# Ten-step normalisation in place of the five-step one, with its own order of work, in a convolution and matching-pursuit kernel

## The chip, the cores and the metric

One core of a Trainium2 chip. The metric is the device time of one launch in microseconds. A core has TensorE (PE), VectorE (DVE), ScalarE (ACT), GpSimd (POOL) and SyncE (SP), each with an instruction list of its own; they meet only at semaphores.

## The reference, cut to what matters

```python
# x: (16, 64, 128, 128) float32
x = x + conv3x3_circular(_gn(x), weight)            # 64 -> 64 channels
x = x + sparse_code(_gn(x), dictionary)             # 4x4 patches of 64 channels: 1024 values, 1024 patches an image

def _gn(v, G=32, eps=1e-5):                         # groups of two channels
    m, s = mean(g), var(g)                          # over the group's 2 x 128 x 128 values
    return (g - m) / sqrt(s + eps)

# sparse_code: five rounds of matching pursuit for each patch
#   h = D^T x; k = 1..5: pick the atom with the largest |h|, extend the Cholesky factor by the
#   Gram entries of the atoms picked so far, h = h_bar - (coefficients @ Gram rows)
#   result = D @ coefficients
```

## The kernel before

An image is worked on in three consecutive periods. In period `i` the kernel convolves image `i` (8 blocks, `convolve(i, 0..7)`, each 18 matmul steps into `conv_ps`), correlates its patches with the 512 normalised atoms (8 tiles of 128 patches, `correlate`; tiles 0 to 3, group 0, in period `i`; tiles 4 to 7, group 1, in period `i + 1`), runs the five search rounds of each group over periods `i`, `i + 1` and `i + 2`, and reconstructs in period `i + 2` (two groups of eight blocks, `recon(i, 2, g, d)`). A period has ten **units**, entries `(periods back, group, round)` of `UNITS`: 0 (1,0,0), 1 (2,1,3), 2 (1,0,1), 3 (2,1,4), 4 (1,0,2), 5 (1,1,0), 6 (1,0,3), 7 (1,1,1), 8 (1,0,4), 9 (1,1,2). The last period, the **tail**, has twelve units and plans of its own.

A unit on each engine:

- ScalarE makes the absolute value of `h` for four tiles (line 644, "score"), the third and fourth only after VectorE has found the maximum of the first and second. The scores of unit n have the **places** 4n to 4n + 3.
- VectorE first extends the factor (`algebra`) and subtracts the projections (`project`, lines 880 and 888, two pairs of tiles), and then searches: `max` (line 771), `aim`, `max_index` (line 780), then writes which atoms, signs and Gram cells (lines 783 to 793).
- GpSimd gathers the Gram cells (line 489, four for each atom chosen before) and four Gram rows (line 501), in the order of the units, and adds a finished half of a group to the output (`add`, line 509) at the units named in `ADD_PLAN`.

Everything else is slotted in by tables written by hand. `SCALAR_PLAN[p]` lists what ScalarE does behind the score of place p; `VECTOR_PLAN[p]` what VectorE does inside unit p // 4, in steps of half a place (0 at its start, 1 and 1.5 after the first and second pair of `project`, 2 after the maxima, 2.5 after `aim`, 3 after `max_index`, 3.5 at its end). The names in them:

- `ev c`: eviction of convolution block c with its sum (line 595); the next block waits for it, since both halves of `conv_ps` are rewritten.
- `z t`, `h t`: normalised patches of tile t, into two buffers in turn (line 577); eviction of its correlation (line 588).
- `st p`: statistics (line 369): parts 0 to 8 for the next image's first norm, parts 9 to 17 for the second norm of this image.
- `oh g, t, j`: one-hot row of atom j of tile t (lines 553 and 556, four buffers, each free again when VectorE has used it); `ce g, pair`: VectorE adds them up to coefficient rows of two tiles (lines 676 and 682); `ct g, t`: eviction of their transposes (`turn` on TensorE, line 934; line 540).
- `re g, d`: eviction of a reconstruction into `rb` (line 565). For d = 0 and 4 it waits until the half that stood in `rb` has been added to the output.
- `co g`: the last row of the factor and the coefficients (VectorE, `coefficients`).
- `gn n`, `rt n`: VectorE's and ScalarE's steps of norm n, which is 0 for the image before its convolution and 1 after it.

TensorE's order is written out in `period`. Correlations and reconstructions share three PSUM banks (`gen_ps0` to `gen_ps2`); `BANKS` says which bank holds which, in order, and `room` waits for the eviction of the one before in the same bank.

Norm n before: ScalarE leaves mean, variance and three signed copies of the mean in `mv[:, n, :]`; `average` multiplies all five columns by the group matrix (line 1012); `root` on ScalarE makes variance and its root from the result in three instructions (lines 618 to 622); `gn_part` 1 on VectorE turns that into factor and offset in five (lines 696 to 705) and, for norm 0, scales the weights (lines 714 to 723); `bias` on TensorE (line 1017) makes the shift, which VectorE copies in `gn_part` 2 (line 729). `convolve(i, 0)` waits for the weights and for the shift.

## Time and profile before

| | us |
|---|---|
| median of 3 runs | 3541.99 (3540.3 to 3543.6) |
| the profiled run | 3542.37 |
| span of its profile | 3540.5 |
| TensorE busy | 3021.8 |
| VectorE busy | 2554.9 |
| ScalarE busy | 2387.1 |
| GpSimd busy | 1893.8 |

The span runs from the first to the last instruction in the trace; the run's own time is 1.9 us longer. An engine is busy while an instruction of it works; the rest is waiting. "[9.94 <-DVE ce L682]" in a row says that the engine had been idle for 9.94 us and that VectorE's instruction on `ce`, line 682, ended the wait. A wait costs time only where nothing else could have gone on.

### The profile page before, as it was taken

How to read it: one execution, taken by the hardware profiler on the slowest of the kernel's cores; microseconds unless marked ns; L12 is line 12 of the kernel's file. 1: busy time of each engine (PE TensorE's matmuls, PEld its weight loads, DVE VectorE, ACT ScalarE, POOL GpSimd, SP SyncE). 2: the span in 40 equal slices, each digit the busy share in tenths (PEclk: the TensorE clock that was granted, in tenths of full speed). 3: DMA queues.
4: the chain of work that ended last, by engine and by line, in shares of the span. 5: the costliest groups of instructions: out<-in, count | busy, mean ns of one | idle time of the engine just before them, and what ended most of it. 6: DMA issues, size and time to landing. Idle time of an engine off the chain costs nothing.

```text
span 3540.5 us, 34757 instructions
## 1 busy us (share of the span) xinstructions
PE 3021.8 (85%) x9424; PEld 1282.2 (36%) x9424; DVE 2554.9 (72%) x6469; ACT 2387.1 (67%) x3923; POOL 1893.8 (53%) x1869
## 2 busy tenths in 40 slices
PE   4995989799898989989898998989898998985547
PEld 1442334343333334333333433333343433332213
DVE  1137877878687787868778776878868687887881
ACT  3555776858677685767768676767867676755534
POOL 0016565646656564655646465555656555566661
PEclk9997999999999999999999999999999999997768
DMA  3433444435254443534444353445434443432232
GB/s 116 154 129 99 153 134 139 130 90 188 63 160 129 145 131 82 192 71 162 115 146 139 90 176 79 153 115 164 123 106 158 91 163 93 129 97 67 52 72 48
DMA packets 130515, 428.37 MB, mean 121 GB/s; under 512 B 55696, under 2 KB 55952, under 8 KB 105616
## 3 DMA queue, kind: packets, MB, share of 16 engines
q0 software_dynamic: 91776, 204.20, 23.6%
q1 hardware_dynamic: 38544, 221.96, 17.5%
q8 instruction: 76, 1.25, 0.1%
q14 instruction: 119, 0.97, 0.1%
HBM read 289.70 MB, written 136.31 MB: 120 GB/s over the span
## 4 chain that ended last, share of the span: by engine, by line
PE 46%; DVE 17%; ACT 11%; issue 10%; DMA 7%; POOL 7%; ACTq 0%; POOLq 0%; DVEq 0%
PE gen_ps L963 19%; PE gen_ps L975 16%; DVE u L880 7%; POOL v L489 6%; PE conv_ps L1031 6%; DMA y_rows<-rb 4%; ACT hot L553 4%; PE conv_ps L1038 3%; DMA v<-gram_rows,cell 3%; DVE top L771 3%; DVE h L888 2%; DVE idx L780 2%; ACT score L644 2%; ACT rb L565 1%; ACT junk_sums L369 1%
## 5 line engine op out<-in xcount | busy, mean ns | idle before, releaser
L489 POOL DMA_INDIRECT v<-gram_rows,cell x1280 | 1277.1, 998 | 882.9 <-DVE cell L789 512.9
L963 PE MATMUL gen_ps<-ct,dt 128*128 128x512 f32 x2048 | 960.2, 625 | 79.8 <-ACT rb L565 57.6
L975 PE MATMUL gen_ps<-dn,z 128*128 128x512 f32 x2048 | 915.5, 600 | 71.6 <-ACT h L588 51.3
L1031 PE MATMUL conv_ps<-xh,wc 128*128 128x512 f32 x1536 | 688.3, 596 | 46.2 <-ACT xa L595 45.2
L501 POOL DMA_INDIRECT u<-marked_rows,chosen x504 | 540.3, 1072 | 309.5 <-DVE chosen L785 160.6
L771 DVE MAX8 top<-score 128x8 f32<-128x512 f32 x640 | 420.5, 691 | 297.5 <-ACT score L644 281.7
L963 PEld LDWEIGHTS gen_ps<-ct,dt 128*128 128x128 f32 x2048 | 402.1, 200 | 603.6 <-issue 574.3
L975 PEld LDWEIGHTS gen_ps<-dn,z 128*128 128x128 f32 x2048 | 385.8, 192 | 568.6 <-issue 524.2
L644 ACT ACTIVATE score<-h 128x512 f32<-128x512 f32 x640 | 374.0, 600 | 296.2 <-DVE top L771 163.9
L880 DVE SCALAR_TENSOR_TENSOR u<-u,nl 128x512 f32<-128x512 f32 x748 | 512.1, 747 | 9.0 <-DMA u<-marked_rows,chosen 5.7
L565 ACT ACTIVATE rb<-gen_ps 128x512 f32<-128x512 f32 x256 | 274.4, 1100 | 273.3 <-PE gen_ps L963 186.3
L682 DVE SCALAR_TENSOR_TENSOR ce<-hot,xc,ce 128x512 f32<-128x512 f16 x512 | 363.9, 747 | 112.2 <-ACT hot L556 111.1
L1031 PEld LDWEIGHTS conv_ps<-xh,wc 128*128 128x128 f32 x1536 | 286.5, 189 | 407.7 <-issue 406.4
L780 DVE FIND_INDEX8 idx<-h 128x8 uint32<-128x520 f32 x640 | 432.1, 694 | 0.0
L553 ACT ACTIVATE hot<-count,which 128x512 f16<-128x512 f16 x512 | 360.7, 704 | 33.8 <-DVE ce L682 33.8
L556 ACT ACTIVATE hot<-hot,plus_minus 128x512 f16<-128x512 f16 x512 | 369.5, 722 | 16.6
L1040 PE MATMUL conv_ps<-xh,wq 64*64 64x512 f32 x1536 | 359.3, 597 | 0.0
L1038 PE MATMUL conv_ps<-xh,wq 64*64 64x512 f32 x1536 | 359.2, 597 | 0.0
L888 DVE SCALAR_TENSOR_TENSOR h<-u,na,h 128x512 f32<-128x512 f32 x504 | 352.9, 745 | 7.4 <-DMA u<-marked_rows,chosen 5.8
L577 ACT ACTIVATE z<-xa,fac 128x512 f32<-128x512 f32 x256 | 297.7, 1264 | 69.9 <-PE gen_ps L975 66.2
L934 PE MATMUL ct_ps<-ident,ce 128*128 128x128 f32 x512 | 99.1, 326 | 259.4 <-DVE ce L682 189.8
L595 ACT ACTIVATE xa<-conv_ps,shift 128x1024 f32<-128x1024 f32 x128 | 141.6, 1106 | 181.6 <-PE conv_ps L1040 181.6
(104 smaller groups left out, 1840.3 us busy)
## 6 DMA issues: line engine op xcount, KB each, us to landing
xh<-x_paired SPq DMA_DIRECT2D x128, 650.0 KB, 4.0
xa<-x_pairs SPq DMA_DIRECT2D x64, 1024.0 KB, 6.2
y_rows<-xa SPq DMA_DIRECT2D x64, 1024.0 KB, 5.1
y_rows<-rb POOLq DMA_DIRECT2D x64, 1024.0 KB, 8.5
v<-gram_rows,cell POOLq DMA_INDIRECT x1280, 2.4
u<-marked_rows,chosen POOLq DMA_INDIRECT x504, 3.9
dn<-atoms SPq DMA_DIRECT2D x1, 2048.0 KB, 11.5
gram_rows<-u POOLq DMA_DIRECT2D x4, 256.0 KB, 2.4
```

The costliest lines, as they stand in the source:

```text
L489: pool.indirect_dma_start(v[:, g, k - 1, j, t:t + 1], None, cells, bass.IndirectOffsetOnAxis(ap=cell[:, g, k // (KMAX - 1), j, t:t + 1], a ...
L501: pool.indirect_dma_start(kept(img, g, k, t), None, marked, bass.IndirectOffsetOnAxis(ap=chosen[:, g, t:t + 1], axis=0))\
L553: act.activation(place, count[:], ACT.Abs, bias=which[:, img % 2, g, j, t:t + 1], scale=-1.0)\
L644: act.activation(score[t % 2][:], h[:, g * T + t, 0:ATOMS], ACT.Abs).then_inc(score_ready[g], 1)
L771: dve.max(top8[:, t, :], score[t % 2][:]).then_inc(top_found[g], 1)
L780: dve.max_index(idx8[:, t, :], h[:, g * T + t, ATOMS:HW], h[:, g * T + t, :]).then_inc(located[g], 1)
L880: dve.scalar_tensor_tensor(kept(img, g, k, t), kept(img, g, j, t), nl[:, g, k - 1, j, t:t + 1], kept(img, g, k, t), ALU.mult, ALU.add).the ...
L888: dve.scalar_tensor_tensor(hh, kept(img, g, k, t), na[:, g, k, t:t + 1], hh, ALU.mult, ALU.add)\
L963: last = pe.matmul(to[:], dt_[:, a, d, :], ct[:, a, :], start=(a == 0), stop=(a == NA - 1))
L975: last = pe.matmul(to[:], z[:, t % 2, d // PATCH, d % PATCH, :], dn[:, d, :], start=(d == 0), stop=(d == ND - 1))
L1031: pe.matmul(conv_ps[:, a], wc[:, tap, a * CIN:a * CIN + P], rows[:, a + 1:a + 2 * CP:2, tap:tap + W], start=(tap == 0), stop=False)
L1038: pe.matmul(conv_ps[above, a], wq[second, tap, :], rows[second, a:a + 2 * CP - 1:2, tap:tap + W], start=False, stop=(tap == TAPS - 1))
```

## The change

It replaces the five-column average by three matmuls of one column, and moves nearly everything that the tables place.

- Norm n: `average` multiplies the mean alone. VectorE (part 1) copies the group mean, subtracts it and forms variance plus squared difference; `spread`, a new matmul, averages that; VectorE (part 2) adds eps; `root` is one square root on ScalarE; VectorE (part 3) makes factor, offset and, for norm 0, the weights in five instructions; part 4 is the copy of the shift. The input `avg_in` and the tiles `mv` and `gsc` shrink, `eps` goes, and the semaphore `gn_ready` is replaced by a first step of `gn_step`.
- Plans: `VECTOR_PLAN`, `SCALAR_PLAN`, `ADD_PLAN`, their tail versions and `BANKS` are other tables. For VectorE the steady order is the same but for the parts of the norms, `co 1` (23.5 for 24) and `ce 0, 1`, which stands behind `aim` instead of ahead of it.
- TensorE: convolution 7 stands between reconstructions (0,4) and (0,5), and the end of the period is in another order, with `spread` in it and `bias` last.

The core of the diff:

```diff
-GN_STEPS = 5
-GN_SUMS = (2, 1)
-GN_ROOT = 3
+GN_STEPS = 10
+GN_SUMS = (3, 2)
 VECTOR_PLAN = {
-    30: [("ce", 1, 1), ("gn", 1, 1)], 37.5: [("gn", 0, 1)], 39.5: [("gn", 0, 2)],
+    30: [("ce", 1, 1), ("gn", 1, 1)], 31: [("gn", 1, 2), ("gn", 1, 3)], 37: [("gn", 0, 1)],
+    39.5: [("gn", 0, 2), ("gn", 0, 3), ("gn", 0, 4)],
...
 SCALAR_PLAN = {
-    0: [("oh", 0, 0, 1), ("oh", 0, 1, 1)],
+    0: [("z", 4), ("oh", 0, 0, 1)],
...
-    27: [("re", 0, 4), ("st", 16), ("st", 17), ("ct", 1, 0)],
+    27: [("re", 0, 4), ("ev", 7), ("re", 0, 5), ("re", 0, 6), ("re", 0, 7), ("ct", 1, 0)],
...
 ADD_PLAN = {
-    4: [(0, 0)], 6: [(0, 1)], 7: [(1, 0)], 9: [(1, 1)],
+    4: [(0, 0)], 5: [(0, 1)], 7: [(1, 0)], 9: [(1, 1)],
 TAIL_VECTOR_PLAN = {
-    1.5: [(2, ("co", 0))], 10: [(2, ("ce", 0, 0))], 13.0: [(2, ("ce", 0, 1))], 24: [(2, ("co", 1))],
-    27: [(2, ("ce", 1, 0))], 33.0: [(2, ("ce", 1, 1))], 43.5: [(1, ("co", 0)), (1, ("ce", 0, 0))],
+    0: [(2, ("co", 0))], 10: [(2, ("ce", 0, 0))], 17.5: [(2, ("ce", 0, 1))], 21.5: [(2, ("co", 1))],
+    22.5: [(2, ("ce", 1, 0))], 27: [(2, ("ce", 1, 1))], 43.5: [(1, ("co", 0))], 44: [(1, ("ce", 0, 0))],
...
 BANKS = (
-    (("corr", 4), ("corr", 7), ("re", 0, 2), ("re", 0, 5), ("re", 1, 0), ("re", 1, 2), ("re", 1, 4), ("re", 1, 7)),
-    (("corr", 5), ("re", 0, 0), ("re", 0, 3), ("re", 0, 6), ("re", 1, 1), ("re", 1, 3), ("re", 1, 5), ("corr", 2)),
-    (("corr", 6), ("re", 0, 1), ("re", 0, 4), ("re", 0, 7), ("corr", 0), ("corr", 1), ("re", 1, 6), ("corr", 3)),
+    (("corr", 4), ("corr", 7), ("re", 0, 2), ("re", 0, 5), ("re", 1, 0), ("corr", 0), ("re", 1, 4), ("re", 1, 6)),
+    (("corr", 5), ("re", 0, 0), ("re", 0, 3), ("re", 0, 6), ("re", 1, 1), ("re", 1, 3), ("re", 1, 5), ("corr", 3)),
+    (("corr", 6), ("re", 0, 1), ("re", 0, 4), ("re", 0, 7), ("re", 1, 2), ("corr", 1), ("corr", 2), ("re", 1, 7)),
...
             def root(image, n):
-                gs = gsc[n]
-                act.wait_ge(gn_sum[n], at(image, GN_SUMS[n], 1))
-                act.activation(gs[:, 6:9], st_ps[:, 5 * n + 2:5 * n + 5], ACT.Square, accum_out=gs[:, 0:1]).then_inc(gn_root[n], 1)
...
+                act.wait_ge(gn_step[n], at(image, GN_STEPS, 5))
+                act.activation(gsc[n][:, 4:5], gsc[n][:, 3:4], ACT.Sqrt).then_inc(gn_root[n], 1)
...
                 if part == 1:
...
+                    dve.wait_ge(gn_sum[n], at(i, GN_SUMS[n], 1))
+                    dve.tensor_copy(gs[:, 0:1], st_ps[:, 3 * n:3 * n + 1]).then_inc(gn_step[n], 1)
                     after(2)
+                    dve.tensor_tensor(gs[:, 1:2], mv[:, n, 0:1], gs[:, 0:1], ALU.subtract).then_inc(gn_step[n], 1)
+                    after(3)
+                    dve.scalar_tensor_tensor(gs[:, 2:3], gs[:, 1:2], gs[:, 1:2], mv[:, n, 1:2], ALU.mult, ALU.add)\
                         .then_inc(gn_step[n], 1)
+                elif part == 2:
+                    dve.wait_ge(gn_sum[n], at(i, GN_SUMS[n], 2))
+                    dve.tensor_scalar(gs[:, 3:4], st_ps[:, 3 * n + 1:3 * n + 2], GN_EPS, None, ALU.add).then_inc(gn_step[n], 1)
+                elif part == 3:
+                    dve.wait_ge(gn_root[n], at(i, 1, 1))
+                    dve.reciprocal(gs[:, 5:6], gs[:, 4:5]).then_inc(gn_step[n], 1)
...
+            def spread(i, n):
+
+                pe.wait_ge(gn_step[n], at(i, GN_STEPS, 4))
+                pe.matmul(st_ps[:, 3 * n + 1:3 * n + 2], avg[:], gsc[n][:, 2:3], start=True, stop=True).then_inc(gn_sum[n], 1)
```

Where the tables move work, the order of instructions shows it. TensorE, end of a steady period, before: from reconstruction (1,6) to the next image's first convolution (lines 963 reconstruction, 975 correlation, 1017 bias, 1031 convolution).

```order
L963 MATMUL gen_ps2<-ct,dt 128x512 x4
L963 MATMUL gen_ps0<-ct,dt 128x512 x4
L975 MATMUL gen_ps1<-dn,z 128x512 x8
L1017 MATMUL conv_ps<-fac0,tap_sum 128x1
L975 MATMUL gen_ps2<-dn,z 128x512 x8
L1031 MATMUL conv_ps<-xh,wc 128x512 x6
```

The same place now (lines 968 reconstruction, 980 correlation, 1022 spread, 1027 bias, 1041 convolution).

```order
L980 MATMUL gen_ps2<-dn,z 128x512 x8
L968 MATMUL gen_ps0<-ct,dt 128x512 x4
L1022 MATMUL conv_ps<-gsc0,avg 128x1
L980 MATMUL gen_ps1<-dn,z 128x512 x8
L968 MATMUL gen_ps2<-ct,dt 128x512 x4
L1027 MATMUL conv_ps<-fac0,tap_sum 128x1
L1041 MATMUL conv_ps<-xh,wc 128x512 x6
```

Between bias and convolution stood a correlation; now they are neighbours. VectorE at the end of unit 9, before: the shift alone (line 729) between `hsel` and the solution of group 0.

```order
L789 SCALAR_TENSOR_TENSOR cell<-which 128x8
L793 SCALAR_TENSOR_TENSOR hsel<-pos,top 128x4
L729 COPY shift<-conv_ps 128x1
L802 TENSOR_TENSOR tmp_last<-nl,v 128x12
```

And now, in the same place:

```order
L798 SCALAR_TENSOR_TENSOR hsel<-pos,top 128x4
L698 TENSOR_SCALAR gsc<-conv_ps 128x1
L701 RECIPROCAL gsc<-gsc 128x1
L703 TENSOR_TENSOR gsc<-gsc 128x1
L705 TENSOR_SCALAR gsc<-gsc 128x1
L708 RECIPROCAL fac<-gsc 128x1
L710 TENSOR_SCALAR fac<-gsc,fac 128x1
L719 TENSOR_SCALAR wc<-taps,fac 128x3x128
L720 TENSOR_SCALAR wc<-taps,fac 128x3x64
L721 TENSOR_SCALAR wq<-taps,fac 128x192
L725 TENSOR_TENSOR wc<-wc,ident 64x2x64
L728 TENSOR_TENSOR wc<-wc,ident 64x64
L734 COPY shift<-conv_ps 128x1
L807 TENSOR_TENSOR tmp_last<-nl,v 128x12
```

Factor and weights of norm 0 have moved from unit 9's middle to its end. ScalarE behind eviction 3, before (`z 6`, a one-hot pair, `st 10`, `st 11`, `z 7`):

```order
L595 ACTIVATE xa0,sums1<-conv_ps,shift 128x2x512
L577 ACTIVATE z<-xa1,fac1 128x128x4 x2
L553 ACTIVATE hot<-count,which 128x512
L556 ACTIVATE hot<-hot,plus_minus 128x512
L369 ACTIVATE few1,minus_shift1<-sums1 128x4
L369 ACTIVATE junk_sums,sums1<-xa0,minus_shift1 128x1024 x2
L577 ACTIVATE z<-xa1,fac1 128x128x4 x2
```

And now the rows from unit 3's last score to `z 7` (line 639 score, 371 statistics):

```order
L639 ACTIVATE score1<-h 128x512
L553 ACTIVATE hot<-count,which 128x512
L556 ACTIVATE hot<-hot,plus_minus 128x512
L540 ACTIVATE ct<-ct_ps 128x4x128
L588 ACTIVATE h<-gen_ps0 128x512
L553 ACTIVATE hot<-count,which 128x512
L556 ACTIVATE hot<-hot,plus_minus 128x512
L371 ACTIVATE junk_sums,sums1<-xa0,minus_shift1 128x1024
L577 ACTIVATE z<-xa1,fac1 128x128x4 x2
```

`z 7` stood ahead of unit 3's scores and now stands behind them.

## Rows read from the trace of the kernel before

**Rows 1.** The page: busy time, share of the span, instructions of each engine.
```profile
PE 3021.8 (85%) x9424; PEld 1282.2 (36%) x9424; DVE 2554.9 (72%) x6469; ACT 2387.1 (67%) x3923; POOL 1893.8 (53%) x1869
```
**Rows 2.** By stretch: us, busy PE PEld DVE ACT POOL, clock, DMA share, GB/s.
```profile
1783.50:1988.20 204.70, 185.26 (x583) 78.49 (x582) 158.15 (x402) 148.07 (x244) 118.10 (x117) 0.96 0.44 129
...
3216.50:3540.50 324.00, 169.96 (x385) 75.70 (x384) 218.37 (x528) 165.38 (x237) 164.29 (x160) 0.75 0.28 62
```
**Rows 3.** Timeline of TensorE (start, us, line, shapes, idle before), 1900 to 1940.
```profile
1901.20 7.03 PE L963 MATMUL gen_ps<-ct,dt 128*128 128x512 f32 x16
1910.16 5.37 PE L963 MATMUL gen_ps<-ct,dt 128*128 128x512 f32 x8 [1.93 <-ACT rb L565]
...
1926.93 1.12 PE L934 MATMUL ct_ps<-ident,ce 128*128 128x128 f32 x4 [9.94 <-DVE ce L682]
...
1930.78 8.84 PE L963 MATMUL gen_ps<-ct,dt 128*128 128x512 f32 x16 [0.69 <-ACT ct L540]
```
**Rows 4.** The same timeline at the end of that period: bias, correlation 3, convolution 0.
```profile
1980.97 0.38 PE L1017 MATMUL conv_ps<-fac,tap_sum 64*128 64x1 f32 x2
1981.28 7.13 PE L975 MATMUL gen_ps<-dn,z 128*128 128x512 f32 x16
1988.25 1.03 PE L1031 MATMUL conv_ps<-xh,wc 128*128 128x512 f32 x2
```
**Rows 5.** Timeline of VectorE, 1969 to 1990: factor, shift, solution, first maximum.
```profile
1969.10 0.16 DVE L696 RECIPROCAL gsc<-gsc 128x1 f32<-128x1 f32 x1 [10.52 <-ACT gsc L622]
...
1970.00 0.22 DVE L705 TENSOR_SCALAR fac<-conv_ps,fac 128x1 f32<-128x1 f32 x1
...
1981.97 0.17 DVE L802 TENSOR_TENSOR tmp_last<-nl,v 128x12 f32<-128x12 f32 x1 [0.34 <-issue]
...
1986.08 0.16 DVE L863 TENSOR_TENSOR xc<-xc,tmp 128x4 f32<-128x4 f32 x1
1989.64 0.70 DVE L771 MAX8 top<-score 128x8 f32<-128x512 f32 x1 [3.40 <-ACT score L644]
```
**Rows 6.** Timeline of ScalarE, 1829 to 1832: a one-hot pair, eviction 3.
```profile
1829.22 0.71 ACT L553 ACTIVATE hot<-count,which 128x512 f16<-128x512 f16 x1
1829.96 0.72 ACT L556 ACTIVATE hot<-hot,plus_minus 128x512 f16<-128x512 f16 x1
...
1831.06 1.10 ACT L595 ACTIVATE xa<-conv_ps,shift 128x1024 f32<-128x1024 f32 x1
```
**Rows 7.** Timeline of ScalarE: a `z`, and the last two scores of unit 3.
```profile
1803.48 2.36 ACT L577 ACTIVATE z<-xa,fac 128x512 f32<-128x512 f32 x2
...
1853.42 1.20 ACT L644 ACTIVATE score<-h 128x512 f32<-128x512 f32 x2 [3.76 <-DVE top L771]
```
**Rows 8.** Timelines: GpSimd's last cell gather of unit 1; VectorE's first use.
```profile
1832.58 0.95 POOL L489 DMA_INDIRECT v<-gram_rows,cell  x1 [0.30 <-issue]
...
1840.00 0.17 DVE L802 TENSOR_TENSOR tmp<-nl,v 128x8 f32<-128x8 f32 x1 [5.08 <-DMA v<-gram_rows,cell]
```
**Rows 9.** Timelines: GpSimd's add of half (0,0); ScalarE's `re 0,4` behind its landing.
```profile
1899.43 0.98 POOL L509 DMA_DIRECT2D y_rows<-rb  x1 [4.66 <-ACT rb L565]
...
1908.93 1.08 ACT L565 ACTIVATE rb<-gen_ps 128x512 f32<-128x512 f32 x1 [3.16 <-DMA y_rows<-rb]
```
**Rows 10.** Busy time by stretch: behind the 2 us wait; around the 2.4 us one.
```profile
1910.30:1913.70 3.40, 3.40 (x5) 1.34 (x6) 2.73 (x4) 2.18 (x10) 2.77 (x3) 0.51 0.15 55
...
1855.60:1862.40 6.80, 4.41 (x29) 1.89 (x22) 6.58 (x21) 6.55 (x13) 2.72 (x3) 1.00 0.57 205
```
**Rows 11.** Timeline of TensorE in the period of image 1: correlations 1 and 2.
```profile
325.87 16.01 PE L975 MATMUL gen_ps<-dn,z 128*128 128x512 f32 x32 [15.26 <-ACT h L588]
```
**Rows 12.** Timelines in the tail: GpSimd's first gather of unit 9; VectorE's wait for them.
```profile
3385.53 0.95 POOL L489 DMA_INDIRECT v<-gram_rows,cell  x1 [1.18 <-DVE cell L789]
...
3407.40 0.17 DVE L802 TENSOR_TENSOR tmp_last<-nl,v 128x12 f32<-128x12 f32 x1 [6.23 <-DMA v<-gram_rows,cell]
```

More of the change, by code:

```diff
@@ L441, in first_statistics @@
                 statistics(act, 0, 0, part)
[L443 removed]
+        setup(nc, ctx, sem, w_taps, atoms, ident_in, avg_in, dn, taps, tap_sum, ones, count, ident, avg, plus_minus, rd,
               atoms_in, first_image, first_rows, first_statistics)
@@ L912, in period @@
                     search(i - back, g, k, between)
-            for part in (1, 2):
+            for part in (1, 2, 3, 4):
                 gn_part(0, 0, 0, part)
@@ L1093, in period @@
                     recon(i, 2, 0, 4)
-                    turn(i - 2, 1, 0)
+                if own:
+                    convolve(i, 7)
+                if p:
                     recon(i, 2, 0, 5)
@@ L1097, in period @@
                     recon(i, 2, 0, 7)
+                    turn(i - 2, 1, 0)
+                    turn(i - 2, 1, 1)
                 if own:
@@ L1100, in period @@
                 if p:
-                    turn(i - 2, 1, 1)
                     turn(i - 2, 1, 2)
                     turn(i - 2, 1, 3)
+                if own:
+                    spread(i, 1)
+                if p:
                     recon(i, 2, 1, 0)
                     recon(i, 2, 1, 1)
+                    recon(i, 2, 1, 2)
                 if own:
@@ L1117, in period @@
                     recon(i, 2, 1, 5)
-                    recon(i, 2, 1, 6)
-                    recon(i, 2, 1, 7)
                 if own:
                     correlate(i, 0, 2)
+                if p:
+                    recon(i, 2, 1, 6)
+                if here[-1]:
+                    spread(i + 1, 0)
+                if own:
+                    correlate(i, 0, 3)
+                if p:
+                    recon(i, 2, 1, 7)
                 if here[-1]:
                     bias(i + 1, 1 - par)
-                if own:
-                    correlate(i, 0, 3)
             def tail(i):
                 correlate(i, 1, 4)
+                turn(i - 2, 0, 0)
                 correlate(i, 1, 5)
-                turn(i - 2, 0, 0)
                 turn(i - 2, 0, 1)
-                turn(i - 2, 0, 2)
                 correlate(i, 1, 6)
                 correlate(i, 1, 7)
+                turn(i - 2, 0, 2)
                 turn(i - 2, 0, 3)
@@ L1181, in _ @@
             average(0, 0)
+            spread(0, 0)
             bias(0, 0)
@@ L1185, in _, with setup @@
             tail(images)
-def setup(nc, ctx, sem, w_taps, atoms, ident_in, avg_in, dn, taps, tap_sum, ones, count, ident, avg, eps, plus_minus, rd,
+def setup(nc, ctx, sem, w_taps, atoms, ident_in, avg_in, dn, taps, tap_sum, ones, count, ident, avg, plus_minus, rd,
           atoms_in, first_image, first_rows, first_statistics):
```

63 lines of the change are left out of this document (23 added, 40 removed), and 98 rows, old and new, of tables (SCALAR_PLAN, TAIL_SCALAR_PLAN, VECTOR_PLAN).

## The prediction

> **What bounds the kernel now.** I read the busy shares first, then one image in the steady state, then TensorE's idle stretches in it, and last who fed them. TensorE is busy 85% of the span, VectorE 72%, ScalarE 67% [rows 1]. One steady period (from the first convolution of an image to that of the next) takes 204.7 us, and TensorE works 185.3 us of it [rows 2]; there are 14 of them. Before them stand the periods of images 0 and 1, behind them the tail of 324.0 us, in which TensorE works 170.0 us [rows 2]. So TensorE sets the steady pace, less its waits. Below, +n is n us after the start of the period that begins at 1783.45.
>
> The waits stand close together. After the reconstructions of group 0 TensorE waits 1.93 us for a bank (`re 0,4` not yet evicted); the block behind it takes 5.37 us where others take 3.5, since the clock has fallen. Then the turns wait 9.94 us for the coefficients of the second pair, and the next two reconstructions take 8.84 us where two take 7.0 [rows 3]. From the end of reconstruction (0,7) to the start of (1,0) pass 15.4 us (1915.4 to 1930.8). Everywhere else in the period TensorE idles under 1 us at a time, but for one wait of 2.4 us.
>
> **The normalisation itself.** Per image and norm the change takes three small ScalarE instructions and the 128x3 one away, and adds five small VectorE ones of 0.16 to 0.22 us [rows 5], a matmul of the size of the average (0.3 us on TensorE) and two more crossings between engines. Bare arithmetic is about 1 us for VectorE and 0.3 us for TensorE per norm, and ScalarE gains about 0.8 us. What counts is where the steps stand.
>
> Norm 1 (of the image after its convolution) runs inside the 15.4 us hole, so I walk the hole again. Reconstruction (0,7) ends at T. Its eviction now stands ahead of `ct 1,0`: the scores of unit 7 start at T+1.4 instead of T+0.7. Statistics 16 and 17, which ran ahead of the hole, now cost ScalarE 2.6 us in it; the one-hot pair `oh 1,3,2` (1.4 us) and `re 0,5` have left it. The last two one-hot tiles are ready at T+10.8 and T+12.6, the coefficients at T+13.4, the last turn and copy end at T+15.3, `spread` passes at T+14.7, and (1,0) starts at T+15.35. So the hole stays 15.4 us; VectorE comes out about 3 us later, but what follows waits for tile 0's correlation in both orders, so I cost that at nothing (cover: `z 2` cannot start before that correlation ends, at T+34.5).
>
> Norm 0 (of the next image) now: VectorE waits 10.52 us for ScalarE's root at 1969.10 [rows 5]. In the new order its first part only needs the average, long since there; the wait goes. What is late next is the second half: scores 38 and 39 stand behind `h 2` and `re 1,6`, the search ends some 6.4 us after reconstruction (1,6), then root, factor and weights end after 9.6 us; TensorE meanwhile has correlation 3 (7.0 us) and reconstruction (1,7) (3.5 us) = 10.5 us. It fits with 0.9 us for the weights and 2.4 us for `bias`. But bias is now the last thing ahead of the convolution, and the shift is copied behind it: 0.15 + 0.15 for the extra matmuls and 0.35 for the copy. Before, bias had a correlation of 7 us as cover [rows 4]. From T to the next convolution: 72.9 us become 73.4.
>
> **The start of the period.** VectorE stands at the shift until +0 and only then solves group 0's coefficients (4.3 us; from 1981.97 to 1986.2 before, ahead of the period) [rows 5]. It used to idle 3.40 us there [rows 5], so of 4 us lag 0.5 us are left after the first search. One-hot tiles: one is made ahead of eviction 0 where three were, at 1.38 us each; the coefficients of the first pair end at +19.8 instead of +18.2. VectorE is then 1.6 us late through units 1 to 3. The wait for gathered cells (5.08 us) [rows 8] does not absorb it, since the cells are asked for 1.6 us later too.
>
> On ScalarE seven one-hot pairs instead of five (one of them held 1.0 us before) stand between unit 2's last score and eviction 3: scores end 1.8 us later, and 2 x 1.38 - 1.0 us are added. Eviction 3 started at +47.6 [rows 6] and now starts at +51.2. Convolution 4 needs it and started at +49.3 without a wait; now it waits 3.5 us, to +52.5. `z 7` was ready at +57.3 in the old list; now it stands behind unit 3's scores, `oh 1,0,2`, `ct 0,2`, `h 4`, `oh 1,1,2` and statistics 13 (together 5.0 us). Those scores started at +70.0 [rows 7], now +71.6 to +72.8; `z 7` (2.3 us [rows 7]) is ready at +80.1. Correlation 7 started at +77.0; now it waits 3.5 us and starts at +80.2.
>
> **What is given back.** From there the old order had 43.8 us of work plus a turn 0.5, the wait 1.93 and the slow block 1.9. The new one puts convolution 7 between reconstructions 4 and 5. Then `re 0,4` is the only tight eviction: `re 0,3` at +116.7, its add lands 9.5 us later (that is what `re 0,4` waited for before, 3.16 us at 1908.93) [rows 9], so `re 0,4` ends at +127.4, and (0,7) may start at +127.5, just when TensorE gets there. So T = +80.2 + 7.0 + 43.8 = +131.0, against +131.9 before.
>
> The period without clock effects: 131.0 + 73.4 = 204.4, against 204.8.
>
> **The clock.** At the 2 us wait the granted clock read 0.51 in the next 3.4 us (the 1.2 GHz level), and such a fall follows that wait in 10 of the 14 periods; around the 2.4 us wait at 1858 it stayed 1.00, in all of them [rows 10]. One fall costs 1.9 us (5.37 against 3.5) [rows 3]. The old fall goes with its wait; that is in the sum. Two new waits of 3.5 us arise. A fall behind the first is absorbed by the second; one behind the second moves T. I take half a fall, +0.9. The Trainium skill ("TensorE: Matmul & The Clock Gate", section "HAM oscillation — how this bites in real kernels") says of a kernel whose engine waits for data in each step that the clock drops each time and the return is paid again each time; the trace bears that out at the long wait of each period and not at the 2.4 us one. By the page each new wait would bring a fall: that is rival A.
>
> **Start and tail.** Image 0: `spread` and the eps step lengthen the chains, about +2 us. Image 1: TensorE waits 15.26 us for `h 0` ahead of the second correlation [rows 11], because tiles 0 and 1 share a bank. In the new bank table tile 1 takes bank 2 and tile 0 bank 0, so one correlation (7.0 us) moves into that wait: -7.0, less 0.4 for the shift. Start together -4.6. Tail: the second half of image 14's coefficients moves from units 6 and 8 to units 5 and 6. GpSimd's gathers of unit 5 are asked for behind 12.4 us of VectorE work that stood behind them, and units 7 and 9 wait for cells: the search of unit 9, which ended at 3384.9 and releases 16 gathers and then everything to the end [rows 12], comes 5 us later. Bounds: -4.5 (a wait for `h` in unit 4 that goes) and +12. I take +5.
>
> **Sum.** 14 x (204.4 + 0.9 - 204.8 = +0.5) = +7.0; start -4.6; tail +5: +7.4. The span 3540.5 becomes 3547.9; its run took 3542.4, 1.9 more, and the median of three is 3542.0, so 3550 us.
>
> **Rivals.**
> A, both clocks fall. Each period 1.9 instead of 0.9 behind the second wait and no relief: +1.4 per period, +20 in all, 3562. For it: a 2 us wait already did it in 10 of 14. Against: the first fall shortens the second wait to 1.7 us.
> B, ScalarE has no slack. From reconstruction (0,2) to `re 0,4` it has 19.6 us of work in 20.7, and the add of (0,1), one unit earlier in GpSimd's list, now holds unit 6's twelve gathers until `re 0,7` is out: they start at +133.4 instead of +126.9. The last cell took up to 6.5 us to be used [rows 8], so unit 8's algebra comes at +155.4, 5 us behind VectorE. I found it covered by `z 2` and by the 5 us after which `h 0` is first needed; a second such delay is not. If one of the two costs 3 us a period: +42, 3584.
> C, faster. The lag of 1.6 us does not arise (VectorE idles 2 to 5 us in units 0 to 3, which my walk fills too strictly), both waits shrink to under 2 us, no clock falls, and the old fall and bank wait are gone all the same: 202.8 a period, 28 us less, 3514.
> D, nothing moves: every loss is covered by the 15.4 us hole; 3542.
>
> **Chances.** Forecast 0.40, A 0.15, B 0.12, C 0.25, D 0.08. The forecast's own spread is about 12 us either way. A measurement can tell about 0.2% (7 us): below 3535 is faster, above 3549 slower. Of the forecast 0.22 lies within, 0.16 above, 0.02 below; of A 0.13 above; D within. Faster 0.27, same 0.32, slower 0.41. Range: C at the low end, B at the high one, 3512 to 3590.
>
> **What would show it.** The wait of 10.5 us before the factor of norm 0 gone, and a short wait of VectorE at the shift in its place; TensorE idle 3 to 4 us ahead of convolution 4 (for eviction 3) and ahead of correlation 7 (for `z 7`), and none ahead of reconstruction (0,7); the hole still 15 to 16 us; in image 1 the second correlation ahead of the long wait. I am wrong if the steady period differs from 205.3 by over 1.5 us, or if TensorE waits over 1 us at `bias` or the first convolution, which would mean that the search of unit 9 ends later than I walked it.

## The result, and the profile after

| | before | after |
|---|---|---|
| median of 5 runs, us | 3542.79 (3540.3 to 3543.6) | 3558.77 (3555.2 to 3562.0) |
| ratio | | 1.0046, 95% interval 1.0034 to 1.0057 |
| the profiled run, us | 3542.37 | 3555.88 |
| its span, us | 3540.5 | 3553.6 |

The changed kernel is slower by 0.46%, 16 us in the medians and 13.1 us in the two profiled spans (the run that was profiled is 2.9 us below the median of its five). By period (from the first convolution of one image to that of the next), in us:

| | before | after | difference | forecast |
|---|---|---|---|---|
| up to image 0's first convolution | 41.4 | 40.9 | -0.5 | |
| image 0 | 138.0 | 142.9 | +4.9 | +2 |
| image 1 | 169.7 | 162.0 | -7.7 | -6.6 |
| images 2 to 14, 13 periods | 2663.2 | 2675.8 | +12.6 | +6.5 |
| image 15 and the tail | 528.2 | 532.0 | +3.8 | +5.5 |

The first of the 13 went from 205.7 to 208.0. The others lay between 204.0 and 205.7; now nine take 204.8 to 205.1 and three 207.5 to 207.8.

The page's line of busy times, after, answers to [rows 1]; each engine does nearly what it did:

```profile
PE 3062.6 (86%) x9488; PEld 1307.6 (37%) x9488; DVE 2581.6 (73%) x6596; ACT 2368.8 (67%) x3795; POOL 1860.6 (52%) x1869
```

Busy time by stretch (columns as in [rows 2]): the first 6.8 us of a convolution 4 with a fallen clock, of a correlation 7 with one, of a convolution 4 without, and a whole steady period.

```profile
1633.80:1640.60 6.80, 6.79 (x9) 2.89 (x10) 2.63 (x16) 6.40 (x13) 5.20 (x6) 0.56 0.93 316
1250.00:1256.80 6.80, 6.80 (x11) 2.96 (x12) 5.89 (x11) 6.74 (x14) 5.28 (x6) 0.70 0.48 156
1221.20:1228.00 6.80, 6.80 (x28) 2.78 (x32) 2.54 (x16) 6.40 (x13) 5.25 (x6) 1.00 0.92 315
1581.40:1786.30 204.90, 187.55 (x587) 80.19 (x587) 159.97 (x411) 147.11 (x237) 115.80 (x117) 0.95 0.43 129
```

**The two kinds of period.** Timeline of TensorE in a period of 205.0 us, which begins at 1581.4 (lines 1041 convolution, 980 correlation):

```profile
1633.81 8.37 PE L1041 MATMUL conv_ps<-xh,wc 128*128 128x512 f32 x12 [3.09 <-ACT xa L595]
1644.86 7.13 PE L980 MATMUL gen_ps<-dn,z 128*128 128x512 f32 x16
...
1661.89 2.41 PE L980 MATMUL gen_ps<-dn,z 128*128 128x512 f32 x5 [0.97 <-ACT z L577]
```

and in one of 207.8 us, which begins at 1168.8:

```profile
1221.16 5.40 PE L1041 MATMUL conv_ps<-xh,wc 128*128 128x512 f32 x12 [3.09 <-ACT xa L595]
1229.23 7.13 PE L980 MATMUL gen_ps<-dn,z 128*128 128x512 f32 x16
...
1249.98 9.16 PE L980 MATMUL gen_ps<-dn,z 128*128 128x512 f32 x16 [4.58 <-ACT z L577]
```

Both wait 3.09 us ahead of convolution 4, at +52.4. In the first the clock falls: the whole convolution takes 11.1 us (1633.81 to 1644.86) where the second needs 8.1, and TensorE comes 3 us later to correlation 7, for which it would have had to wait anyway. In the second the clock stays at 1.00, the wait for `z 7` is 4.58 us, and the clock falls there, where nothing absorbs it: 9.16 us for a correlation of 7.1. With the 0.7 us by which `z 7` itself is later there (+81.2 for +80.5), that is the 2.8 us between the kinds.

**The hole.** TensorE's timeline around the end of reconstruction (0,7), at 1712.7 (+131.3), answers to [rows 3]:

```profile
1704.82 7.89 PE L968 MATMUL gen_ps<-ct,dt 128*128 128x512 f32 x18
1712.54 0.60 PE L939 MATMUL ct_ps<-ident,ce 128*128 128x128 f32 x4
1714.41 0.63 PE L939 MATMUL ct_ps<-ident,ce 128*128 128x128 f32 x4 [1.26 <-ACT ct L540]
1719.47 0.59 PE L1017 MATMUL conv_ps<-mv,avg 128*128 128x1 f32 x2 [4.44 <-ACT mv L416]
1724.36 1.12 PE L939 MATMUL ct_ps<-ident,ce 128*128 128x128 f32 x4 [4.30 <-DVE ce L677]
1726.25 1.09 PE L939 MATMUL ct_ps<-ident,ce 128*128 128x128 f32 x4 [0.78 <-DVE ce L677]
1727.13 0.43 PE L1022 MATMUL conv_ps<-gsc,avg 128*128 128x1 f32 x2
1728.03 8.21 PE L968 MATMUL gen_ps<-ct,dt 128*128 128x512 f32 x14 [0.47 <-ACT ct L540]
```

From the end of (0,7) to the start of (1,0) pass 15.3 us, as in the rows of before (1915.53 to 1930.78 in [rows 3]; the prediction's 15.4 is 0.1 high). The single wait of 9.94 us is cut in two by the average, 4.44 and 4.30 us; `spread` stands at the hole's end.

**Image 1.** TensorE's timeline there (answers to [rows 11]): the second correlation now follows the first at once, at 316.37, and only the third waits for an `h`.

```profile
306.58 9.82 PE L980 MATMUL gen_ps<-dn,z 128*128 128x512 f32 x16 [6.02 <-ACT z L577]
316.37 7.11 PE L980 MATMUL gen_ps<-dn,z 128*128 128x512 f32 x16
326.67 9.99 PE L980 MATMUL gen_ps<-dn,z 128*128 128x512 f32 x16 [3.19 <-ACT h L588]
```

**What I had not foreseen** stands in the page's group for the projection. Idle time ahead of line 885 (880 before) over the whole run, and what ended most of it, before and then after:

```profile
L880 DVE SCALAR_TENSOR_TENSOR u<-u,nl 128x512 f32<-128x512 f32 x748 | 512.1, 747 | 9.0 <-DMA u<-marked_rows,chosen 5.7
```

```profile
L885 DVE SCALAR_TENSOR_TENSOR u<-u,nl 128x512 f32<-128x512 f32 x748 | 513.9, 747 | 95.0 <-DMA u<-marked_rows,chosen 92.4
```

One period of it, after. VectorE in unit 3 (the algebra of line 807 is the first use of the gathered cells, line 885 the first of the Gram rows):

```profile
1635.11 0.21 DVE L807 TENSOR_TENSOR tmp<-nl,v 128x8 f32<-128x8 f32 x1 [0.37 <-DMA v<-gram_rows,cell]
...
1642.04 4.07 DVE L885 SCALAR_TENSOR_TENSOR u<-u,nl 128x512 f32<-128x512 f32 x6 [4.90 <-DMA u<-marked_rows,chosen]
```

GpSimd's last cell gather of unit 1 and the first and last of its row gathers:

```profile
1632.63 0.94 POOL L489 DMA_INDIRECT v<-gram_rows,cell  x1 [0.30 <-issue]
1633.88 0.94 POOL L501 DMA_INDIRECT u<-marked_rows,chosen  x1 [0.30 <-issue]
...
1637.62 0.94 POOL L501 DMA_INDIRECT u<-marked_rows,chosen  x1 [0.30 <-issue]
```

SyncE's queue: the store of group 0 of the convolved image to the output, two transfers of 1 MB.

```profile
1633.69 0.82 SPq L472 DMA_DIRECT2D y_rows<-xa  x2
```

Before, VectorE waited 5.08 us for the cells and not for the rows [rows 8], and the same store, SyncE's timeline of before, came at

```profile
1832.28 0.82 SPq L472 DMA_DIRECT2D y_rows<-xa  x2
```

which is beside the last cell gather (1832.58). The store waits for eviction 3. Whatever gathers lie behind that eviction land late: the cells before, the rows after. In the changed kernel the second half of the store lands at +60.1 to +60.2 in nine of the periods of images 3 to 14, and the first projection starts at +60.5 to +60.6; in the other three it lands at +61.1 to +61.3 and the projection starts at +61.2 to +61.4. So the row that is used first lands with the end of the store, not in the middle of it.

**Rival B** can be read here too. GpSimd's last cell gather of unit 6, and VectorE's first use in unit 8:

```profile
1730.42 0.94 POOL L489 DMA_INDIRECT v<-gram_rows,cell  x1 [0.31 <-issue]
...
1732.81 0.17 DVE L807 TENSOR_TENSOR tmp<-nl,v 128x8 f32<-128x8 f32 x1 [1.43 <-DMA v<-gram_rows,cell]
```

The add does hold unit 6's gathers, until +134.0 (forecast +133.4), but their last cell is used at +151.4 and not at +155.4; VectorE waits 1.43 us for it, and from (0,7) to the next convolution pass 73.3 to 73.9 us in all the periods of images 3 to 14, near the 73.4 that was forecast without B. The 3 us a period of rival B are not there.

### The profile page after: what moved, and what is told of

It is laid out like the page before. It is cut to its first block, busy times and chain, and to the rows that moved or that the text cites. A ratio compares the mean times of both kernels' runs of the same rounds, so it can differ in the third digit from the quotient of the medians.

```text
span 3553.6 us, 34884 instructions
## 1 busy us (share of the span) xinstructions
PE 3062.6 (86%) x9488; PEld 1307.6 (37%) x9488; DVE 2581.6 (73%) x6596; ACT 2368.8 (67%) x3795; POOL 1860.6 (52%) x1869
## 4 chain that ended last, share of the span: by engine, by line
PE 51%; DVE 14%; issue 11%; ACT 9%; POOL 9%; DMA 4%; ACTq 0%; POOLq 0%; DVEq 0%; SPq 0%
PE gen_ps L968 22%; PE gen_ps L980 15%; POOL v L489 9%; PE conv_ps L1041 8%; DVE u L885 6%; PE conv_ps L1048 4%; ACT hot L553 4%; DMA u<-marked_rows,chosen 3%; DVE h L893 2%; DVE idx L785 2%; DVE top L776 2%; ACT score L639 1%; ACT z L577 1%; ACT junk_sums L371 1%; ACT ct L540 1%
## 5 line engine op out<-in xcount | busy, mean ns | idle before, releaser
L968 PE MATMUL gen_ps<-ct,dt 128*128 128x512 f32 x2048 | 945.0, 616 | 65.5 <-ACT rb L565 56.2
L980 PE MATMUL gen_ps<-dn,z 128*128 128x512 f32 x2048 | 926.7, 606 | 50.4 <-ACT z L577 39.9
L1041 PE MATMUL conv_ps<-xh,wc 128*128 128x512 f32 x1536 | 722.2, 621 | 84.3 <-ACT xa L595 76.9
L501 POOL DMA_INDIRECT u<-marked_rows,chosen x504 | 507.6, 1007 | 305.8 <-DVE chosen L790 156.9
L1041 PEld LDWEIGHTS conv_ps<-xh,wc 128*128 128x128 f32 x1536 | 296.4, 197 | 461.5 <-issue 459.1
L509 POOL DMA_DIRECT2D y_rows<-rb x64 | 63.1, 987 | 366.4 <-ACT rb L565 366.3
```

Of the source, the lines that this page charges most:

```text
L501: pool.indirect_dma_start(kept(img, g, k, t), None, marked, bass.IndirectOffsetOnAxis(ap=chosen[:, g, t:t + 1], axis=0))\
L968: last = pe.matmul(to[:], dt_[:, a, d, :], ct[:, a, :], start=(a == 0), stop=(a == NA - 1))
L980: last = pe.matmul(to[:], z[:, t % 2, d // PATCH, d % PATCH, :], dn[:, d, :], start=(d == 0), stop=(d == ND - 1))
L1041: pe.matmul(conv_ps[:, a], wc[:, tap, a * CIN:a * CIN + P], rows[:, a + 1:a + 2 * CP:2, tap:tap + W], start=(tap == 0), stop=False)
```

## Theories

*Theory.* The order of work costs the time, through the two waits that it makes, ahead of convolution 4 (eviction 3 is late) and of correlation 7 (`z 7` stands behind unit 3's scores), and unit 3's scores are late because the store lies on its Gram rows. *Rivals.* The ten steps cost it; a late eviction 3 alone is what matters; the rows are late for a reason of their own; GpSimd's earlier add holds gathers up (B of the prediction).

## The experiments

**Order or steps.** The kernel before with the tables and TensorE's order of the changed one, and the five-step norms kept.

```diff
 VECTOR_PLAN, SCALAR_PLAN, ADD_PLAN, their tail versions, BANKS, period(): those of the changed kernel, but
-    31: [("gn", 1, 2), ("gn", 1, 3)], 37: [("gn", 0, 1)], 39.5: [("gn", 0, 2), ("gn", 0, 3), ("gn", 0, 4)],
+    31: [("gn", 1, 1)], 39.5: [("gn", 0, 1), ("gn", 0, 2)],
```

> The new tables and TensorE order with the old five-step normalisation (no spread; factor of norm 1 at place 31, factor, weights and shift of norm 0 at 39.5). If the order of work makes the difference, as I hold, this stays within 0.15% of the changed kernel: 3552 to 3560 us, steady periods of 205.0 and 207.7 us, and only image 0's period is shorter, by some 3 us (183.8 - 40.9 = 142.9 in the changed kernel). If the ten steps themselves cost the time, it falls to 3540 to 3546.

Measured: 3550.79 us, ratio to before 1.0025 (1.0015 to 1.0035). That is 1.2 us below the range of the first case and far from that of the second. The 13 steady periods read as in the changed kernel, nine at 204.7 to 205.2, three at 207.7 to 207.9, and the first at 210.7 (208.0). Image 0 takes 137.7 us instead of 142.9, image 1 160.1 instead of 162.0. So of 16 us the order costs 10 (3550.8 against 3540.8 for the kernel before on that chip) and the steps some 4 to 6, 4.3 in the profiled spans: 5.2 us in image 0. The 1.9 us of image 1 come back in image 2 (210.7 for 208.0). In the other steady periods the steps cost nothing. On this chip the kernel before took 2.0 us less than on that of the result, and 1.4 us less on the chip of the store by itself and of the version from the parts; differences to the changed kernel below are uncertain by that much.

**`z 7` earlier**, by one place of unit 3:

```diff
-    13: [("oh", 1, 1, 1)],
-    15: [("oh", 1, 0, 2), ("ct", 0, 2), ("h", 4), ("oh", 1, 1, 2), ("st", 13), ("z", 7), ("h", 5), ("h", 6),
+    13: [("oh", 1, 1, 1), ("z", 7)],
+    15: [("oh", 1, 0, 2), ("ct", 0, 2), ("h", 4), ("oh", 1, 1, 2), ("st", 13), ("h", 5), ("h", 6),
```

> The changed kernel with z 7 moved from place 15 to place 13, where ScalarE idles 4.0 us. Theory (TensorE waits for z 7 ahead of correlation 7): that wait (1.0 us where the clock fell before, 4.6 where it did not) and the fall behind it vanish, steady periods 203 to 204.2 us, total 3533 to 3545. Rival (the reconstructions are held by ScalarE and the add, so it is given back before reconstruction 0,7): 3552 to 3560, with a wait of 1 us or more ahead of (0,7).

Measured: 3532.53 us, 0.9976 (0.9967 to 0.9985). The wait ahead of correlation 7 is gone in all periods, the one of 3.1 us ahead of convolution 4 is left, and periods take 202.4 to 204.8 us (image 2's aside, 208.9). The time is half a microsecond below what was expected, and the periods spread wider on both sides. The wait of 1 us or more ahead of (0,7), the rival's sign, is there in seven of the 12 periods of images 3 to 14 (1.1 to 1.7 us), with no fall behind it.

**Eviction 3 earlier**, behind the one-hot pair `oh 0,3,3`:

```diff
-    11: [("oh", 0, 2, 2), ("oh", 0, 3, 2), ("oh", 0, 2, 3), ("oh", 0, 3, 3), ("oh", 0, 2, 4), ("oh", 0, 3, 4),
-        ("oh", 1, 0, 1), ("ct", 0, 1), ("ev", 3), ("st", 10), ("st", 11), ("st", 12), ("st", 0), ("ev", 4)],
+    11: [("oh", 0, 2, 2), ("oh", 0, 3, 2), ("oh", 0, 2, 3), ("oh", 0, 3, 3), ("ev", 3), ("oh", 0, 2, 4), ("oh", 0, 3, 4),
+        ("oh", 1, 0, 1), ("ct", 0, 1), ("st", 10), ("st", 11), ("st", 12), ("st", 0), ("ev", 4)],
```

> The changed kernel with eviction 3 three one-hot pairs and a copy earlier on ScalarE (4.6 us). The wait of 3.1 us ahead of convolution 4 goes, and the clock fall behind it. Theory (z 7 is the later bound, and the fall ahead of it only fills its wait): correlation 7 starts no earlier, waits 4.6 us in every period, the clock falls behind it in most, all steady periods 207 to 208 us, total 3570 to 3590, so slower than the changed kernel. Rival (the wait before convolution 4 is what costs): 3 us a period less, 3510 to 3520.

Measured: 3545.12 us, 1.0012 (1.0003 to 1.0021): neither of the two. The wait ahead of convolution 4 went, and TensorE waited longer for `z 7` instead, 3.7 to 4.6 us, with a fall of the clock behind it in each of the 12 periods of images 3 to 14:

```profile
1655.58 4.63 PE L980 MATMUL gen_ps<-dn,z 128*128 128x512 f32 x5 [3.78 <-ACT z L577]
```

That much was expected. But this correlation 7 starts at +76.9 to +78.5, not at +80.5, though I had taken the move for one that leaves `z 7` where it was. With eviction 3 the store is issued at +47.7 instead of +52.3, the first of the rows lands at +55.8 in the period of this row, and the projection starts at +57.2 without a wait, instead of at +60.6 after 4.9 us. This is what led to the store.

**Both** edits together, nothing else.

> Both moves. Theory: neither wait nor fall is left up to the reconstructions; steady periods 200.5 to 203 us, total 3495 to 3530, faster than the kernel before. If ScalarE's work from reconstruction (0,2) to re 0,4 and the landing of the add take it back, a wait of 2 to 4 us appears ahead of reconstruction (0,7) with a fall behind it and the total is 3535 to 3550.

Measured: 3493.73 us, 0.9871 (0.9856 to 0.9886), 1.3% faster than before, 1.3 us below the range of the theory. Apart the two edits give 26.2 and 13.7 us against the changed kernel, together 65.0: each alone leaves the other wait, and the clock falls behind that one. With both, none of TensorE's waits between +40 and the hole is over 2.1 us, no clock falls behind them, and correlation 7 starts at +73.0 to +73.9 (image 2 aside). Ahead of reconstruction (0,7) this is left:

```profile
1676.53 3.67 PE L968 MATMUL gen_ps<-ct,dt 128*128 128x512 f32 x8 [1.37 <-ACT rb L565]
```

The block takes 3.67 us, so the clock did not fall; in [rows 3] it did behind 1.93 us. In the kernel before the same wait has both outcomes: with 1.87 to 2.55 us over 14 periods the clock fell behind it in 10, and the four others (1.87, 2.02, 2.08 and 2.28 us) are not the shortest ones.

**The store by itself.** The changed kernel with one thing different: SyncE issues the store of group 0 behind convolution 4. No list of a computing engine is touched.

```diff
-                    if here[0] and (r + 1) % (ROUNDS // GROUPS) == 0:
-                        g = r // (ROUNDS // GROUPS)
-                        sp.wait_ge(x1_ready, at(i, ROUNDS, r + 1))
+                    if here[0] and r in (4, ROUNDS - 1):
+                        g = 0 if r == 4 else 1
+                        sp.wait_ge(x1_ready, at(i, ROUNDS, (g + 1) * (ROUNDS // GROUPS)))
```

> The changed kernel, with the store of group 0 of the convolved image (SyncE, two transfers of 1 MB) issued behind convolution 4 instead of right behind eviction 3; the lists of ScalarE, VectorE and TensorE are untouched. Theory (the store lies on top of unit 3's Gram rows: issued at +52.3 and +52.7, second half landed at +60.1, first projection waiting 4.9 us until +60.6): rows land by +57 to +58, the wait of 4.9 us falls under 1.5 us, z 7 comes 2 to 4 us earlier, the wait ahead of correlation 7 goes (0.97 us in the periods of 205.0, 4.58 us in those of 207.8), the wait of 3.1 us ahead of convolution 4 stays; periods 203.5 to 204.2, time 3541 to 3549. Rival (the rows are late for a reason of their own): the projection still waits over 3.5 us, correlation 7 starts at +80.5 to +81.2 as before, time 3555 to 3562.

Measured: 3516.08 us, 0.9932 (0.9918 to 0.9946), 42.7 us less than the changed kernel. The mechanism is the theory's, the size is more than twice it. SyncE's queue in a period that begins at 1565.2:

```profile
1628.25 1.16 SPq L472 DMA_DIRECT2D y_rows<-xa  x2
```

VectorE in unit 3; the wait of 4.90 us has become 0.24 and 0.62:

```profile
1618.85 0.17 DVE L807 TENSOR_TENSOR tmp<-nl,v 128x8 f32<-128x8 f32 x1 [0.30 <-DMA v<-gram_rows,cell]
1621.08 0.75 DVE L885 SCALAR_TENSOR_TENSOR u<-u,nl 128x512 f32<-128x512 f32 x1 [0.24 <-DMA u<-marked_rows,chosen]
1622.45 3.40 DVE L885 SCALAR_TENSOR_TENSOR u<-u,nl 128x512 f32<-128x512 f32 x5 [0.62 <-DMA u<-marked_rows,chosen]
```

TensorE; the wait ahead of convolution 4 is still there, correlation 7 starts at +77.9 without any:

```profile
1617.61 6.94 PE L1041 MATMUL conv_ps<-xh,wc 128*128 128x512 f32 x12 [3.07 <-ACT xa L595]
...
1643.12 7.03 PE L980 MATMUL gen_ps<-dn,z 128*128 128x512 f32 x16
```

Periods alternate between 202.1 us, as here (the first twelve matmuls of convolution 4 take 6.94 us), and 204.1, where they take as long as at 1633.81 above and correlation 7 starts at +79.2. No period pays for a fall at correlation 7 any more, as the three of 207.5 to 207.8 did, and image 2's 208.0, which had none there, is now 203.9. The periods are 203.2 us in the mean, a little lower than expected; the time expected beside them was reckoned too high, since 13 periods of 203.85 instead of 205.8 are 25 us and not 10 to 18. Of the 39.5 us between the two profiled spans the 13 periods give 34.7, the last stretch 3.8 and image 1 1.4; image 0 takes 0.6 more. Why the two kinds of period alternate, I don't know.

**A version from the parts.** The changed order, both edits, the five-step norms, and the tail tables and tail order of the kernel before.

> The new order of work with the five-step normalisation, eviction 3 and z 7 both earlier, and the tail's tables and tail order of the kernel before. Theory (terms add): from 3493.7 (ten steps, both earlier) 5 us less for the five steps and 4 us less for the old tail: 3482 to 3488, the last stretch (last period's first convolution to the end) 524 instead of 528. Rival (the old tail's gain was not in its tables): the last stretch stays 527.5 to 528.5, time 3487 to 3492.

Measured: 3481.53 us, 0.983 (0.9816 to 0.9843): 1.7% faster than before, 2.2% faster than the changed kernel; the theory held, half a microsecond below its range. The last stretch takes 522.3 us, against 528.0 with both edits alone; the five steps account for 0.4 of that (531.6 against 532.0 in the first experiment), the tail's tables for about 5.

**Six runs that tell little.** On two further chips the kernel before itself took 4113.5 and 4048.4 us; there TensorE stands still inside its blocks, between matmuls that wait for no other engine, as in these rows of the kernel with the later store:

```profile
1707.70 1.01 PE L1041 MATMUL conv_ps<-xh,wc 128*128 128x512 f32 x1 [2.21 <-issue]
1710.51 1.01 PE L1041 MATMUL conv_ps<-xh,wc 128*128 128x512 f32 x1 [1.80 <-issue]
```

What hangs on a microsecond of ScalarE's or TensorE's lead can't be read from them; why these chips do so, I don't know. The later store, the same kernel as above:

> The changed kernel, with the store of group 0 of the convolved image (SyncE, two transfers of 1 MB) issued behind convolution 4 instead of right behind eviction 3; ScalarE's, VectorE's and TensorE's lists are untouched. Theory (the store lies on top of unit 3's Gram rows: store issued at +52.3 and +52.7, second half landed at +60.1, projection waiting 4.9 us until +60.6): rows land by +57 to +58, the wait of 4.9 us falls under 1.5 us, z 7 comes 2 to 4 us earlier, the wait ahead of correlation 7 goes (0.97 us in the periods of 205.0, 4.58 us in those of 207.8), the wait of 3.1 us ahead of convolution 4 stays; periods 203.5 to 204.2, time 3541 to 3549. Rival (the rows are late for a reason of their own, the store only shares the time): the projection still waits over 3.5 us, correlation 7 starts at +80.5 to +81.2 as before, time 3555 to 3562.

4130.81 us, 1.0036 (1.0012 to 1.0061) to before on the same chip; without the changed kernel beside it this decides nothing. The add of half (0,1) back at unit 6 of the changed kernel:

```diff
 ADD_PLAN = {
-    4: [(0, 0)], 5: [(0, 1)], 7: [(1, 0)], 9: [(1, 1)],
+    4: [(0, 0)], 6: [(0, 1)], 7: [(1, 0)], 9: [(1, 1)],
```

> The changed kernel with the add of half (0,1) back at unit 6 of GpSimd's list. Theory (holding unit 6's gathers is covered): 3555 to 3562, within 3 us of the changed kernel. Rival B of the prediction (a delay of 3 us a period comes from there): 3515 to 3530.

4103.52 us, 0.9977 (0.9955 to 1.0). On that chip it is 0.6% below the two other descendants of the changed kernel. So on that chip a share of rival B's mechanism can't be excluded; at full pace the edit was not tried, and what is known there rests on the reading of the changed kernel's trace above. The changed kernel with `TAIL_VECTOR_PLAN`, `TAIL_SCALAR_PLAN`, `TAIL_ADD_PLAN` and TensorE's tail order of the kernel before:

> The changed kernel with the tail's tables and TensorE's tail order of the kernel before. Theory: from the last period's first convolution to the end 532.0 becomes 528 to 529, time 3554 to 3556. Rival (the 3.8 us of the end come from the last steady image and not from the tail's plans): 531 to 532, time 3558 to 3560.

4127.93 us, 1.0039 (1.0014 to 1.0063); the last stretch takes 584.0 us against 585.1 and 583.8 in the two runs beside it, no gain to be seen. The tail's 5 us rest on the version from the parts, where the steps were changed too.

The new bank table in the kernel before, alone and then together with the later store. In both, the end of the third bank is ordered to suit the old TensorE order:

```diff
-    (... ("re", 1, 0), ("re", 1, 2), ("re", 1, 4), ("re", 1, 7)),
-    (... ("re", 1, 1), ("re", 1, 3), ("re", 1, 5), ("corr", 2)),
-    (... ("corr", 0), ("corr", 1), ("re", 1, 6), ("corr", 3)),
+    (... ("re", 1, 0), ("corr", 0), ("re", 1, 4), ("re", 1, 6)),
+    (... ("re", 1, 1), ("re", 1, 3), ("re", 1, 5), ("corr", 3)),
+    (... ("re", 1, 2), ("corr", 1), ("re", 1, 7), ("corr", 2)),
```

> The kernel before with only the bank table of the changed one. Theory: image 1's period falls from 169.7 to about 162.5 (correlation 1 runs inside the wait for h 0), all else stays; 3541 - 7 = 3534 (3531 to 3537). Rival (the gain of image 1 comes from other parts of the new order): image 1's period stays over 168, 3539 to 3543.

> The kernel before with two local edits that show in different periods: the bank table of the changed kernel (image 1's period), and the store of group 0 behind convolution 4 as in the run with the later store (steady periods). Bank table: theory, image 1's period falls from 169.7 to 162 or 163; rival, it stays over 168. Store: theory, VectorE's wait of 5.08 us for cells in unit 3 falls under 1 us here too (its store was issued at +48.8 and +49.2, right on the last cell gather at +49.1), but z 7 stands ahead of unit 3's scores in this list, so the period stays within 1 us of 204.7. Rival: the old kernel pays for the collision as well, and periods fall to 203 or less. Together 3525 to 3536 by the theory; under 3515 by the rival.

4238.06 us, 1.0311 (1.0283 to 1.0339), and 4156.45 us, 1.0276 (1.0244 to 1.0309). Both are misses, and for a reason that both traces show. TensorE's waits of the second, us in total, times, longest (the first has 123.3 us in 26 such waits):

```profile
PE gen_ps L975 <- ACT rb L565: 120.2, 28, 5.8
```

Two correlations a period now stand close behind a reconstruction of their own bank and wait until it is evicted: 120 us in the list, against 108 us that the kernel lost. A bank table belongs to one order of TensorE. So the 7.7 us of image 1 were not taken apart; that they come from the banks rests on the row at 316.37, and on image 1's 159.5 to 162.0 us in all seven full-pace runs of the new table. Of the store in the old kernel this answers only in part: VectorE's waits for cells of the kind of [rows 8] sum to 26.3 us in the second run and 56.2 in the first (another chip); what that is worth on the old path stays open.

> The best version so far (new order, five-step norms, eviction 3 and z 7 earlier, old tail) with the store of group 0 behind convolution 4. Theory (there the store at +47.7 still delays the cells of unit 3 by 0.7 to 2 us, but nothing of TensorE's waits for unit 3's scores any more): periods 200 to 201, time 3470 to 3481. Rival (the later store collides with what comes behind, loads of the next image and gathers of unit 4): 3483 to 3495.

4050.81 us, 1.0004 (0.9987 to 1.0022). Whether the later store adds anything to the best version stays open too.

## Why the prediction came out as it did

I forecast 3550 us against 3542, that is +7.4 us; it became +13.1 in the profile and +16 in the medians. The sign was right, and so were the two waits as the cause, and the range held. But one step was wrong, and it was luck that another, which I had left out, made up for it.

**Right, with sizes.** Eviction 3 starts at +51.1 (forecast +51.2) and convolution 4 at +52.4 after 3.09 us (+52.5, 3.5; from +49.3 to +52.5 my own figures make 3.2). `z 7` ends at +80.4 (+80.1), correlation 7 starts at +80.4 to +81.2 (+80.2). Reconstruction (0,7) ends at +131.3 (+131.0) with no wait ahead of it, so the fall of [rows 3] is gone. The hole stays. The wait of 10.52 us of [rows 5] is gone, and at the shift VectorE waits 1.58 us, while TensorE waits 0.37 us at the first convolution:

```profile
1786.03 0.16 DVE L734 COPY shift<-conv_ps 128x1 f32<-128x1 f32 x1 [1.58 <-PE conv_ps L1027]
...
1786.29 3.25 PE L1041 MATMUL conv_ps<-xh,wc 128*128 128x512 f32 x7 [0.37 <-issue]
```

From (0,7) to that convolution pass 73.6 us (73.4). Image 1 gave 7.7 us (6.6). VectorE has four more instructions for each norm and image, not the five that I counted (6596 for 6469 in all); nothing hung on that.

**The step that failed: the price of a gather in [rows 8].** I read there that the last cell takes 6.5 us from the end of its issue to its use, held this for the time of a gather, and concluded that in unit 3 the algebra moves with its request, from +56.6 to +58.2. Counted from the start of the issue it is 7.4 us (1832.58 to 1840.00). The algebra now starts at +53.7, 2.5 us after the start of the last gather's issue (1632.63 to 1635.11), though that gather was issued 2.1 us later than before (+51.2 for +49.1). The page of before had the usual price, the median from issue to landing over all 1280 cell gathers, 2.4 us:

```profile
v<-gram_rows,cell POOLq DMA_INDIRECT x1280, 2.4
```

The other 4.9 us were the price of the store beside the gather. With the store 3.5 us later (+52.3 for +48.8) it is paid at the rows, 4.90 us. VectorE's first projection of unit 3 started at +58.6 before; my walk puts it at +60.2, and it came at +60.6. That the two errors cancel here is luck, and it is why all numbers behind it came out right. The Trainium skill ("DMA: Bandwidth & Descriptors", section "Queues, rings and completion order") says that a transfer engine with work from several queues takes from them in turn, a packet at a time. That the row gathers get a share of the engines while the store runs can't be read from the trace; what it shows is that the first row comes only with the end of the store (used at +60.6, the store's second half landed at +60.1), 8.2 us after the row's issue. With the store out of the way it is used 3.4 us after its issue (+55.8 for +52.4).

The run with the later store shows what becomes of the kernel where nothing lies on those gathers: periods of 202.1 and 204.1 us and 3516 us in all. Rival C had 202.8 us a period and 3514 us, but its reason was another, and the closeness is chance. Its reason, "the lag of 1.6 us does not arise", is false: the coefficients of the first pair end at +19.8, as in my walk, and the last cells of unit 1 are asked for 2.1 us late. The lag ends one step later, in the wait for those cells, of which I wrote that it does not absorb it (5.08 us before, 0.37 now). Nor are C's other conditions met in the run with the later store, where the wait ahead of convolution 4 stays at 3.07 us and the clock falls behind it. The change moves an eviction, and the prediction forgot whom that eviction releases on SyncE's queue. Rival B was priced with the same 6.5 us, which put unit 8's algebra 4 us too late.

**The clock was mis-sized.** I took +0.9 a period: half a fall at 1.9 us, the price in [rows 3], and that for the second wait alone. The clock falls behind the wait of 3.1 us in 11 of the periods of images 2 to 14 and costs up to 3.0 us there (11.1 for 8.1); that one is indeed absorbed by the wait for `z 7`. In the two periods where it stays away (207.8 and 207.5) the second wait grows to 4.58 and 3.84 us, and the fall comes behind that, at 2.0 and 2.4 us for the correlation, absorbed by nothing. The third of them (image 14, 207.8) has both falls; it is the only case of rival A. So a fall behind the second wait comes in 3 of 13 and such a period is up to 2.8 us longer, where I had 1 of 2 and 1.9: 0.65 a period, near the 0.9. What the periods of 205.0 have more than the 204.4 of the sum is 0.3 us at the start of correlation 7, 0.2 behind (0,7), and rounding. The mean of the 13 is 205.8, against 205.3 forecast and 204.9 before; image 2's 208.0, which I had not set apart, is 0.2 of that. The Trainium skill ("TensorE: Matmul & The Clock Gate", section "HAM oscillation — how this bites in real kernels") would have a wait of 3 to 5 us in each step bring a fall each time. At 3.1 us the trace agrees mostly, not always; at 3.7 us and more it agrees in all 12 periods of the run with eviction 3 earlier. The shorter waits lie outside the section's case: at 0.7 to 2.1 us, in the run with both edits, no fall followed, and at 1.9 to 2.6 us, in the kernel before, one followed in 10 of 14 periods.

**Image 0 was mis-sized,** +4.9 for +2: by the first experiment the ten steps alone make 5.2. That in image 0 each crossing between engines lies bare, and the two norms have two more each, is my reading of it; it was not taken apart. Image 15 and the tail together took +3.8 for +5.5: the search of unit 9 in the tail ends 4.3 us later (377.1 us behind the last convolved image's first convolution, for 372.8), where I had 5.
